# First attention: the value product of an odd key step issued one step later, ahead of the next even step's

## The chip, the cores and the metric

One core of one Trainium2 chip runs the whole program. The metric is device time in microseconds (us) of one execution.

## What is computed

Two post-norm transformer layers over 2048 tokens of width 512, each an attention and a feed-forward block with a residual sum and a layer norm behind each. The change touches only the first layer's attention: 16 heads of 32 dimensions, causal, softmax over scores.

```python
q = jnp.concatenate([q_sem, q_geo], axis=-1)
k = jnp.concatenate([k_sem, k_geo], axis=-1)
scores = jnp.einsum('bhqd,bhkd->bhqk', q, k).astype(jnp.float32) * scale
scores = jnp.where(causal, scores, jnp.finfo(jnp.float32).min)
attn = jax.nn.softmax(scores, axis=-1).astype(v.dtype)
out = jnp.einsum('bhqk,bhkd->bhqd', attn, v)
```

## The kernel before

`layer0_attention` works on 16 **items**, each one chunk of 512 queries and one group of four heads. Item (c, g) has a **step** for each tile of 128 keys that chunk c may see: 4, 8, 12 or 16 steps, 160 in all, an even number in each item. Items 0 to 3 belong to chunk 0, 4 to 7 to chunk 1, 8 to 11 to chunk 2 and 12 to 15 to chunk 3. In an item full tiles and diagonal tiles alternate at first; a diagonal tile covers 512, 384, 256 or 128 queries and gets a mask matmul (line 843).

A step i has this work:

- `scores`: four matmuls on PE, one a head (line 838), each into one of **three** PSUM banks `stb`. ACT takes the exponential of each (line 702) into `probs`, which has four step buffers. Scores number k wait for the exponential of scores k-3.
- `av`, the value product: four matmuls (line 855) that use 32 of the 128 columns each, side by side, and sum into one bank `avb`. They wait for the step's four exponentials.
- POOL adds the probabilities of an odd step to those of the even step before it (line 668), in two halves, after the even step's `av`.
- `den`, the denominators: four matmuls against ones (line 876) on that sum, for even steps only, in the same shape of 32 columns, into another bank.

Beside this runs the search for each query's largest score, which the softmax subtracts, for items still to come. A `unit` is one matmul (line 817) into one of **three** PSUM banks `sbank`, over 512 keys or, on the diagonal, 128 to 512; DVE reduces it (line 740, or 745 on the diagonal). The matmul of a unit waits until the unit three before it is reduced. A `turn` transposes an item's maxima on PE (line 824) after DVE has finished them (line 752), and takes an `sbank` bank too. There are 640 units; all of them have been issued before item 15, the last item, begins.

`attention0_plan` writes out one list, `order`, and every engine walks it and takes its own entries. It first sets which units and turns stand in the gap behind each of the 640 scores (`in_gap`), by costs and due times. Then it lays out the steps: for step i the scores of heads 0, 1 and 2, each with its gap, then the block of 32-column work, then head 3. Before the change that block is `av` of step i-1 at every i, followed by `den` of step i-3 where i is odd. Six entries `prep` (conversions on ACT and DVE that belong to the next stage) are put in the block's place too, in the first steps of item 15; PE has no work in them.

The lines that set the waits are these.

```python
if k >= 3:
    pe.wait_ge(s["exp_ok"], k - 2)
...
pe.wait_ge(s["exp_ok"], 4 * i + 4)
...
act.wait_ge(s["av_ok"], i - PSLOTS + 1)
```

Of the kernel before, what the change touches and what calls it, by code (L numbers as in the profile page):

```python
# [131 lines left out]
def query_slots(items):  # L132

    slot = [n % (QSLOTS + INX) if n < 2 * NG else (n - 2 * NG) % QSLOTS for n in range(items)]
    old = [max((o for o in range(n) if slot[o] == slot[n]), default=-1) for n in range(items)]
    return slot, old
# [305 lines left out]
def attention0_plan():  # L442


    items = [(c, g) for c in range(NC) for g in range(NG)]
    steps, first, final = [], [], []
    for n, (c, g) in enumerate(items):
        diagonal, full = [c * TC + d for d in range(TC)], list(range(c * TC))
        order = [kt for pair in zip(full, diagonal) for kt in pair] + full[TC:] if c else diagonal
        first.append(len(steps))  # L450
        steps += [(n, kt) for kt in order]
        final.append(len(steps) - 1)
    units = [[(h, t, u) for u in (*range(c), c) for t in range(TC) for h in range(GH)] for c, g in items]

    def width(n, kt):
        return CH - max(0, kt - TC * items[n][0]) * P

    def cost(n, unit):
        h, t, u = unit
        return 151 + (CH if u < items[n][0] else (t + 1) * P)  # L460

    clock, begin = 0.0, []
    gaps = []
    for i, (n, kt) in enumerate(steps):
        if i == first[n]:
            begin.append(clock)
        for h in range(4):
            clock += 0.25 * width(n, kt) * 7.0
            gaps.append((clock, i, h))
    lead = 7500.0  # L470
    q_old = query_slots(len(items))[1]

    loads, last_use = [], {}
    for i, (n, kt) in enumerate(steps):
        last_use[n, kt // TC] = i
    for n, (c, g) in enumerate(items):
        loads += [(n, j) for j in range(c + 1)]
    freed = {}
    for at, (n, j) in enumerate(loads):
        freed[n, j] = last_use[loads[at - KSLOTS]] if at >= KSLOTS else -1  # L480

    done = 0.0
    corners = []
    for n in range(len(items)):
        done += sum(cost(n, x) for x in units[n])
        corners.append((begin[n] - lead, done))
    early = list(range(EARLY))
    here, have = 0.0, corners[early[-1]][1]
    path = [(here, have)]
    while have < corners[-1][1]:  # L490
        slope, to = max(((d - have) / (at - here), n) for n, (at, d) in enumerate(corners) if d > have)
        here, have = corners[to]
        path.append((here, have))

    def when(amount):
        for (a0, h0), (a1, h1) in zip(path, path[1:]):
            if amount <= h1:
                return a0 + (a1 - a0) * (amount - h0) / (h1 - h0)
        return path[-1][0]

    in_gap = [[] for _ in gaps]
    before = []
    amount, at_gap = 0.0, 0
    end_of = {i: max(k for k, gap in enumerate(gaps) if gap[1] == i) for i in range(len(steps))}
    for n in range(len(items)):
        for j, unit in enumerate(units[n]):
            amount += cost(n, unit)
            if n in early:
                before.append(("unit", n, j))
                continue  # L510
            t = when(amount)
            free = max(freed[n, unit[2]], final[q_old[n]] if q_old[n] >= 0 else -1)
            if free >= 0:
                t = max(t, gaps[end_of[free]][0] + 4000.0)
            while at_gap < len(gaps) - 1 and gaps[at_gap][0] < t:
                at_gap += 1
            in_gap[at_gap].append(("unit", n, j))
        if n in early:
            if n > 0:
                before.insert(len(before) - len(units[n]) + 4, ("turn", n - 1))  # L520
            if n == early[-1]:
                before.append(("turn", n))
        else:
            k = at_gap
            while gaps[k][0] < gaps[at_gap][0] + 1500.0:
                k += 1
            in_gap[k].append(("turn", n))

    order = list(before)
    k = 0  # L530
    for i, (n, kt) in enumerate(steps):
        for h in range(4):
            if h == 3 and i > 0:
                order.append(("av", i - 1))
                if 2 <= i - final[-2] < 2 + PREP:
                    order.append(("prep", i - final[-2] - 2))
                if i >= 3 and i % 2:
                    order.append(("den", i - 3))
            order.append(("scores", i, h))
            order += in_gap[k]  # L540
            k += 1
    order += [("av", len(steps) - 1), ("den", len(steps) - 2)]
    return items, steps, first, final, units, loads, last_use, order


def layer0_attention(nc, stage_before, stored, landed, qx, qk_dram, m_dram, xs_dram, acc_dram, token, V, X, hi, lo, qst, consts, early, out_w, first_o):
    items, steps, first, final, units, loads, last_use, order = attention0_plan()
    unit_no, ring, scored = {}, {}, {}
    for at, ev in enumerate(order):
# [2025 lines left out]
```

## Time and profile before

| what | value |
|---|---|
| time, median of 3 runs | 2267.35 us (2264.82 to 2269.28) |
| span of the profiled execution, first to last instruction | 2262.5 us |
| what lies around the span, against the median | 4.85 us |
| PE busy in the span | 2168.5 us, 96% |
| DVE, ACT, POOL busy | 52%, 33%, 30% |
| first attention in the span | some 160 to 740 us |

The profiled execution has a span but no separate time of its own beside it; the three runs lie 2.3 to 6.8 us above its span. A busy PE is an upper bound: matmuls overlap in the records, so the pace of a stretch is read from the starts of its instructions, not from their lengths. Idle time of an engine that is not the bottleneck costs nothing.

### The profile page before, as it was taken

What the parts mean: (1) busy time and instruction counts of PE and PEld (TensorE: products, weight loads), DVE (VectorE), ACT (ScalarE), POOL (GpSimd) and SP (SyncE); (2) the same over time, 40 slices, a digit from 0 to 9 for tenths busy, and PEclk for the clock granted to TensorE, in tenths of its full rate; (3) what the DMA queues carried; (4) which work ended last, traced back from release to release, by engine and by line L of the source; (5) the groups of instructions that cost most, each with busy time, mean ns of one, the idle gap of its engine ahead of it and who ended that gap; (6) DMA issues with size and microseconds to landing.
All of it is one profiled execution on the core that took longest, in us unless ns stands there. A gap on an engine that the chain in (4) does not pass through costs nothing. (4 is left out here: it accounts for less than half of the span.)

```text
span 2262.5 us, 27504 instructions
## 1 busy us (share of the span) xinstructions
PE 2168.5 (96%) x10148; PEld 1493.8 (66%) x10148; DVE 1184.8 (52%) x2325; ACT 752.9 (33%) x1351; POOL 669.7 (30%) x456
## 2 busy tenths in 40 slices
PE   7999999999999899999989899999998999999997
PEld 6866555555553554444467778888887888888886
DVE  5877777776662553222246652322336546554666
ACT  3325555555557322111134321111223211211223
POOL 4354555645556105242223250000003021211200
PEclk9989999999999999999999999999999999999999
DMA  4578345333300615555534460000101010100001
GB/s 180 187 200 197 87 123 129 99 91 72 71 17 21 243 65 218 135 120 90 90 104 149 144 231 25 28 19 19 46 1 56 1 38 19 38 19 20 18 19 56
DMA packets 104605, 197.27 MB, mean 87 GB/s; under 512 B 10385, under 2 KB 27665, under 8 KB 103057
## 3 DMA queue, kind: packets, MB, share of 16 engines
q1 hardware_dynamic: 92064, 162.78, 24.4%
q0 software_dynamic: 11408, 29.69, 5.7%
q10 hardware_dynamic: 1008, 3.15, 0.4%
q8 instruction: 78, 1.28, 0.2%
q14 instruction: 47, 0.38, 0.1%
HBM read 123.82 MB, written 71.75 MB: 86 GB/s over the span
## 5 line engine op out<-in xcount | busy, mean ns | idle before, releaser
L702 ACT ACTIVATE a_probs<-a_stb 128x512 f32<-128x512 f32 (+3 forms) x640 | 309.7, 535 | 241.2 <-PE a_stb L843 126.7
L668 POOL TENSOR_TENSOR a_probs<-a_probs 128x1024 f32<-128x1024 f32 (+3 forms) x158 | 278.0, 1773 | 247.9 <-PE a_avb L855 234.0
L740 DVE TENSOR_REDUCE a_mparts<-a_sbank 128x1 f32<-128x512 f32 x384 | 239.9, 683 | 86.3 <-PE a_sbank L817 86.1
L2215 POOL CAST m_wh<-wst 128x1024 fp32r<-128x1024 f32 x24 | 26.7, 1112 | 716.1 <-POOLq L1532 366.9
L57 PE MATMUL m_gu<-hi,m_wh 128*128 128x512 f32 x512 | 199.7, 390 | 3.5 <-DVE lo L2284 1.9
L59 PE MATMUL m_gu<-hi,m_wl 128*128 128x512 f32 x512 | 199.4, 389 | 0.0
L58 PE MATMUL m_gu<-lo,m_wh 128*128 128x512 f32 x512 | 199.2, 389 | 0.0
L855 PE MATMUL a_avb<-a_probs,V 128*32 128x512 f32 (+3 forms) x1280 | 151.7, 546 | 0.7 <-ACT a_probs L702 0.7
L745 DVE CUSTOM_DVE_ANT_0 a_junk<-a_sbank,hidden 128x128 bf16<-128x128 f32 (+3 forms) x256 | 113.1, 487 | 59.0 <-PE a_sbank L817 57.6
L2294 DVE TENSOR_TENSOR m_h<-m_sg,m_gu 128x512 f32<-128x512 f32 x63 | 43.2, 686 | 190.5 <-ACT m_sg L2245 190.3
L2245 ACT ACTIVATE m_sg<-m_gu 128x512 f32<-128x512 f32 x64 | 38.3, 598 | 261.6 <-PE m_gu L59 261.5
L817 PE MATMUL a_sbank<-hi,q 96*128 96x512 f32 (+3 forms) x304 | 118.7, 412 | 5.9 <-DVE a_mparts L740 4.2
L838 PE MATMUL a_stb<-q,hi 97*128 97x512 f32 (+3 forms) x304 | 121.8, 410 | 1.6 <-ACT a_probs L702 1.1
L1817 ACT ACTIVATE pth<-q_tb 128x512 fp32r<-128x512 f32 x64 | 38.2, 598 | 244.6 <-PE q_tb L2074 244.6
L1954 DVE TENSOR_TENSOR ptl<-q_tb,pth 128x512 fp32r<-128x512 f32 x64 | 44.1, 691 | 143.3 <-ACT pth L1817 143.3
L817 PE MATMUL a_sbank<-lo,q 96*128 96x512 f32 (+3 forms) x288 | 109.4, 405 | 5.4 <-DVE a_mparts L740 3.3
L838 PE MATMUL a_stb<-q,lo 97*128 97x512 f32 (+3 forms) x288 | 110.3, 398 | 2.2 <-ACT a_probs L702 1.9
L57 PEld LDWEIGHTS m_gu<-hi,m_wh 128*128 128x128 f32 x512 | 96.1, 188 | 24.0 <-DVE lo L2284 2.1
L59 PEld LDWEIGHTS m_gu<-hi,m_wl 128*128 128x128 f32 x512 | 96.1, 188 | 20.1
L58 PEld LDWEIGHTS m_gu<-lo,m_wh 128*128 128x128 f32 x512 | 96.1, 188 | 19.9
L1303 POOL DMA_INDIRECT acc<-e_rows_b,X x37 | 57.8, 1563 | 166.1 <-DVE e_rows_b L1427 139.2
L57 PE MATMUL q_vb<-vh,pth 128*128 128x512 f32 x256 | 101.3, 396 | 3.7 <-DMA vl<-v 3.7
(289 smaller groups left out, 4753.7 us busy)
## 6 DMA issues: line engine op xcount, KB each, us to landing
qk<-v_hl SPq DMA_DIRECT2D x32, 512.0 KB, 3.1
hi<-qk SPq DMA_DIRECT2D x60, 256.0 KB, 5.2
lo<-qk SPq DMA_DIRECT2D x60, 256.0 KB, 5.3
wst<-in_w_mlp SPq DMA_DIRECT2D x24, 512.0 KB, 3.5
q<-qk SPq DMA_DIRECT2D x42, 256.0 KB, 5.8
xs<-a_zeros POOLq DMA_DIRECT2D x39, 264.0 KB, 2.7
X<-xs SPq DMA_DIRECT2D x39, 264.0 KB, 2.7
v<-vhl SPq DMA_DIRECT2D x16, 512.0 KB, 4.9
```

The lines of the kernel that those rows point to most:

```text
L57: nc.tensor.matmul(out, wh, xh, start=start, stop=False, skip_group_check=True)
L58: nc.tensor.matmul(out, wh, xl, start=False, stop=False, skip_group_check=True)
L59: return nc.tensor.matmul(out, wl, xh, start=False, stop=stop, skip_group_check=True)
L668: nc.gpsimd.tensor_tensor(probs[:, i % PSLOTS, hs, w0:], probs[:, i % PSLOTS, hs, w0:], probs[:, (i + 1) % PSLOTS, hs, w0:], ALU.add)\
L702: nc.scalar.activation(probs[:, i % PSLOTS, h, w0:], stb[:, k % 3, w0:], ACT.Exp, scale=SCALE0)\
L740: nc.vector.reduce_max(to, sbank[:, b, :], AX).then_inc(s["unit_max"], 1)
L745: nc.vector.tensor_tensor_reduce(out=junk[:, k % 2, 0:w], in0=sbank[:, b, 0:w], in1=hidden[:, CH - w:CH], scale=1.0, scalar=BIG, op0=ALU.a ...
L817: nc.tensor.matmul(bank[:, 0:w], qs[q_slot[n]][0:96, h, t * P:(t + 1) * P], kst[at % KSLOTS][0:96, h, 0:w], start=True, stop=True)\
L838: last = nc.tensor.matmul(stb[:, k % 3, w0:], kst[slot_of[n, kt // TC] % KSLOTS][0:97, h, kt % TC * P:(kt % TC + 1) * P], qs[q_slot[n]][0: ...
L855: last = nc.tensor.matmul(avb[HD0 * h:HD0 * (h + 1), w0:], V[:, kt, g * P + h * HD0:g * P + (h + 1) * HD0], probs[:, i % PSLOTS, h, w0:], ...
L1303: nc.gpsimd.indirect_dma_start(acc_dram[:, :], bass.IndirectOffsetOnAxis(ap=to[:, j:j + 1], axis=0), y[:, j % 2, :], None, compute_op=ALU. ...
L1954: nc.vector.tensor_tensor(ptl[:, 4 * g:4 * g + 4, :].rearrange("p a b -> p (a b)"), tb[:, (g + 1) % 2, :], f32(pth[:, 4 * g:4 * g + 4, :]) ...
```

## The change

In `attention0_plan` the block of step i now depends on whether i is odd. For odd i it holds `av` of step i-2, `av` of step i-1 and `den` of step i-3. For even i it is empty, unless step i-1 is the last of its item: then that step's `av` stands there as before. The counter of gaps is renamed.

```diff
     order = list(before)
-    k = 0
+    gap = 0
     for i, (n, kt) in enumerate(steps):
         for h in range(4):
             if h == 3 and i > 0:
-                order.append(("av", i - 1))
+                if i % 2:
+                    order += [("av", k) for k in (i - 2, i - 1) if k >= 0 and k not in final]
+                elif i - 1 in final:
+                    order.append(("av", i - 1))
                 if 2 <= i - final[-2] < 2 + PREP:
                     order.append(("prep", i - final[-2] - 2))
                 if i >= 3 and i % 2:
                     order.append(("den", i - 3))
             order.append(("scores", i, h))
-            order += in_gap[k]
-            k += 1
+            order += in_gap[gap]
+            gap += 1
```

Of the 80 odd steps 16 are the last of an item, so 64 value products move. Only PE's order changes; DVE, ACT, POOL and the DMA queues have their entries in the order they had. Lines behind the edit stand three higher in the changed kernel: 838 becomes 841, 817 becomes 820, 855 becomes 858, 876 becomes 879.

The first place is PE in item 10, steps 80 to 83, all full tiles. `a_stb` are scores, `a_sbank` units, `a_avb` a value product, `a_den` denominators. Before:

```order
L838 MATMUL a_stb<-q,hi 128x512
L817 MATMUL a_sbank<-hi,q 128x512
L855 MATMUL a_avb<-a_probs,V 32x512 x4
L838 MATMUL a_stb<-q,hi 128x512
L817 MATMUL a_sbank<-hi,q 128x512
L838 MATMUL a_stb<-q,hi 128x512
L817 MATMUL a_sbank<-lo,q 128x512 x2
L838 MATMUL a_stb<-q,hi 128x512
L817 MATMUL a_sbank<-lo,q 128x512
L838 MATMUL a_stb<-q,hi 128x512
L817 MATMUL a_sbank<-lo,q 128x512
L855 MATMUL a_avb<-a_probs,V 32x512 x4
```

After the change, the same stretch of PE's program:

```order
L841 MATMUL a_stb<-q,hi 128x512
L820 MATMUL a_sbank<-hi,q 128x512
L841 MATMUL a_stb<-q,hi 128x512
L820 MATMUL a_sbank<-hi,q 128x512
L841 MATMUL a_stb<-q,hi 128x512
L820 MATMUL a_sbank<-lo,q 128x512 x2
L841 MATMUL a_stb<-q,hi 128x512
L820 MATMUL a_sbank<-lo,q 128x512
L841 MATMUL a_stb<-q,hi 128x512
L820 MATMUL a_sbank<-lo,q 128x512
L858 MATMUL a_avb<-a_probs,V 32x512 x8
L879 MATMUL a_den<-a_probs,a_ones 32x512 x4
```

The first `av` (step 81) has moved behind the second group of scores and units and stands as one block of eight with that of step 82. Between two blocks there are now eight scores and nine units in a row, where there were four and four, then four and five.

The second place is PE in item 15, steps 152 to 155, which has no units. Before:

```order
L838 MATMUL a_stb<-q,hi 128x512 x4
L855 MATMUL a_avb<-a_probs,V 32x512 x4
L838 MATMUL a_stb<-q,hi 128x512 x4
L855 MATMUL a_avb<-a_probs,V 32x512 x4
L876 MATMUL a_den<-a_probs,a_ones 32x512 x4
```

After the change:

```order
L858 MATMUL a_avb<-a_probs,V 32x512 x8
L879 MATMUL a_den<-a_probs,a_ones 32x512 x4
L841 MATMUL a_stb<-q,hi 128x512 x8
L858 MATMUL a_avb<-a_probs,V 32x512 x8
L879 MATMUL a_den<-a_probs,a_ones 32x512 x4
```

Here eight scores follow each other with nothing between them, where there were two groups of four.

## Rows read from the trace of the kernel before

**Rows 1.** The page: span, busy time of each engine, granted TensorE clock in 40 slices.

```profile
span 2262.5 us, 27504 instructions
...
PE 2168.5 (96%) x10148; PEld 1493.8 (66%) x10148; DVE 1184.8 (52%) x2325; ACT 752.9 (33%) x1351; POOL 669.7 (30%) x456
...
PEclk9989999999999999999999999999999999999999
```

**Rows 2.** Busy us of each engine by stretch, then clock, DMA share, GB/s.

```profile
692.00:740.00 48.00, 43.97 (x280) 16.46 (x280) 9.28 (x10) 32.04 (x67) 29.54 (x16) 1.00 0.03 10
200.00:690.00 490.00, 475.01 (x2961) 253.27 (x2964) 340.17 (x809) 273.20 (x569) 272.44 (x184) 1.00 0.38 91
```

**Rows 3.** Waits from 175 to 735 us: total us, times, longest.

```profile
DVE a_mparts L740 <- PE a_sbank L817: 86.1, 78, 2.7
...
PEld a_sbank L817 <- DVE a_mparts L740: 19.8, 47, 1.4
```

**Rows 4.** Timeline of PE, item 10: start, us, instructions.

```profile
466.05 0.49 PE L817 MATMUL a_sbank<-hi,q 96*128 96x512 f32 x1
466.48 1.07 PE L855 MATMUL a_avb<-a_probs,V 128*32 128x512 f32 x8
467.36 1.04 PE L876 MATMUL a_den<-a_probs,a_ones 128*32 128x512 f32 x8
468.33 0.50 PE L838 MATMUL a_stb<-q,hi 97*128 97x512 f32 x1
468.67 0.40 PE L817 MATMUL a_sbank<-hi,q 96*128 96x512 f32 x1
...
470.07 0.39 PE L817 MATMUL a_sbank<-hi,q 96*128 96x512 f32 x1
470.39 1.07 PE L855 MATMUL a_avb<-a_probs,V 128*32 128x512 f32 x8
471.39 0.50 PE L838 MATMUL a_stb<-q,hi 97*128 97x512 f32 x1
...
472.91 0.50 PE L817 MATMUL a_sbank<-lo,q 96*128 96x512 f32 x1
...
473.50 0.50 PE L817 MATMUL a_sbank<-lo,q 96*128 96x512 f32 x1
473.94 1.06 PE L855 MATMUL a_avb<-a_probs,V 128*32 128x512 f32 x8
...
475.79 0.50 PE L838 MATMUL a_stb<-q,hi 97*128 97x512 f32 x1
```

**Rows 5.** Timeline of DVE in the same stretch.

```profile
469.10 2.48 DVE L740 TENSOR_REDUCE a_mparts<-a_sbank 128x1 f32<-128x512 f32 x4 [1.31 <-PE a_sbank L817]
472.16 3.08 DVE L740 TENSOR_REDUCE a_mparts<-a_sbank 128x1 f32<-128x512 f32 x5 [0.57 <-PE a_sbank L817]
```

**Rows 6.** Groups of full width from 175 to 735 us: count, busy us, mean ns.

```profile
L702 ACT ACTIVATE a_probs<-a_stb 128x512 f32<-128x512 f32 x443 | 240.0, 600 | 136.0 <-PE a_stb L838 107.7 <-PE a_stb L843 25.5
L740 DVE TENSOR_REDUCE a_mparts<-a_sbank 128x1 f32<-128x512 f32 x384 | 239.9, 683 | 86.3 <-PE a_sbank L817 86.1
```

**Rows 7.** Timeline of PE in item 15.

```profile
729.22 0.98 PE L838 MATMUL a_stb<-q,hi 97*128 97x512 f32 x3
730.42 0.50 PE L838 MATMUL a_stb<-q,hi 97*128 97x512 f32 x1 [0.21 <-ACT a_probs L702]
730.85 1.06 PE L855 MATMUL a_avb<-a_probs,V 128*32 128x512 f32 x8
...
735.31 0.50 PE L838 MATMUL a_stb<-q,hi 97*128 97x512 f32 x1
```

**Rows 8.** Timeline of ACT in item 15.

```profile
729.76 2.07 ACT L702 ACTIVATE a_probs<-a_stb 128x512 f32<-128x512 f32 x4 [1.41 <-PE a_stb L838]
```

**Rows 9.** Timeline of POOL in item 15.

```profile
728.61 4.71 POOL L668 TENSOR_TENSOR a_probs<-a_probs 128x1024 f32<-128x1024 f32 x2 [1.38 <-PE a_avb L855]
```

**Rows 10.** One line's instructions: the `prep` conversions on ACT, ns min/median/max.

```profile
L718 ACT ACTIVATE woh<-V x4: 632/652/653, 694.4 to 702.8; 128x512 fp32r<-128x512 f32 x4
```

## The prediction

> **What bounds the kernel now.** I read the page first, then the busy time by stretch, then the waits, then the timelines of two places. The page shows PE busy for 96% of the span and the clock granted nearly in full [rows 1]. By stretch, in the first attention the clock is 1.00, PE is busy 475 of 490 us between 200 and 690 us, DVE 340, ACT 273 and POOL 272 [rows 2]. So PE sets the pace there, but DVE, at 69%, is not far behind. The waits say the same: DVE waits for units (86 us in all), while PE's weight loads waited 20 us for reductions, in 47 places [rows 3]. Those 47 places matter below: with three banks DVE already stops PE where units come close together. In the last item the picture is another: no units, ACT busy 32 of 48 us [rows 2], and PE waits for an exponential at the fourth scores of every step [rows 7].
>
> **What a seam costs.** The change removes no instruction. It removes 64 seams, the places where PE goes from full-width matmuls to 32-column ones and back. In item 10 a seam is read from starts [rows 4]. Six matmuls go from 468.67 to 470.07: 0.233 us each. From the last unit to the value product it is 0.32 (470.07 to 470.39), 0.09 more. A value product that scores follow takes 1.00 (470.39 to 471.39); one that 32-column work follows takes 0.88 (466.48 to 467.36); 0.12 more. The first scores behind a block hold the next unit off for 0.34 (468.33 to 468.67), 0.11 more. Together **0.32 us a seam**, and 64 of them are 20.5 us, the ceiling of what can come.
>
> The Trainium skill, "TensorEngine Tiling (Array Packing)", section "Tiling Modes", says that changing the tiling mode drains the TensorE. The row's 0.32 us agrees with that. By that rule alone the change would take off the whole 20.5 us.
>
> **What the seam was hiding.** While PE runs a block, DVE and ACT empty the three banks each has ahead. The change puts eight scores, with all their units, in one run. A unit goes with each scores at 2 x 0.233 = 0.467 us, and a reduction follows the one before it after (2.48 - 0.68)/3 = 0.60 us [rows 5, 6]. So a run of full units falls behind by 0.13 us a unit, and three banks cover only the first few.
>
> *Nine full units (item 10, steps 81 to 83).* The run begins at 468.33, its first four units at 468.67 to 470.07 as before, the first reduction at 469.10 [rows 4, 5]. Reduction n ends at 469.10 + 0.60(n-1) + 0.68, and the unit three later starts 0.06 us after that (before: reduction 2 of the second run ends at 472.16 + 0.60 + 0.68 = 473.44, its unit starts at 473.50). Unit 5 would come at 470.07 + 0.47 = 470.54, reduction 2 allows 470.44: no wait. Unit 6 would come at 471.01, allowed 471.04. From here DVE sets the pace: unit 7 at 471.64, 8 at 472.24, 9 at 472.84. Behind a delayed unit the block starts 0.44 later (473.50 to 473.94), not 0.32: 473.28. The merged block is 0.88 + 0.88 + 0.97 (467.36 to 468.33): the next scores at 476.01. Before they came at 475.79 [rows 4]. So this merge is **0.22 us slower**, although its seam is gone.
>
> *Eight full units.* The same walk ends with unit 8 at 472.24, the block at 472.68, the next scores at 475.41. Before, two groups of four without a wait are 468.33 + 2.06 + 1.00 + 2.06 + 1.85 = 475.30. So 0.11 us slower.
>
> *Few or narrow units.* With five or fewer there is no wait, and the merge gives 0.32.
>
> **The sum.** I counted in the order what each of the 64 merged runs of eight scores holds, a narrow unit by its share of 512.
>
> - 21 runs hold less than seven full units' worth. Between -0.32 and nothing; narrow diagonal scores, which let PE run faster than DVE and ACT, are in 20 of them, so I take half: -0.16 x 21 = -3.4 us.
> - 36 hold seven or more, nine of them with a turn, at which PE waits for the maxima anyway, so that a late DVE is partly paid already. Between -0.32 and +0.22; most are like the eight-unit walk, the ones with a turn or narrow units below it. I take +0.07: +2.5 us.
> - 7 lie in the last item. Eight scores from 729.22: the first exponential starts at 729.76, four take 2.07 with the last one 0.60 long, so 0.49 apart [rows 6, 8]; the fifth ends at 729.76 + 1.96 + 0.60 = 732.32. Scores 8 wait for it, plus 0.06 (730.36 to 730.42 before): 732.38. The block starts 0.43 later [rows 7], 732.81, and the next scores at + 2.73 = 735.54, against 735.31 before: +0.23 each, 1.6 us. In addition three of the six `prep` conversions, 0.65 us each on ACT [rows 10], now stand in the middle of a run where ACT sets the pace, no block being there to cover them. Between nothing and 0.65; I take 0.5: +1.5 us. Together +3.1.
>
> The sum is -3.4 + 2.5 + 3.1 = **+2.2 us**. It is made against the profiled span of 2262.5, which has no other time of its own on the page; the median of the runs is 4.85 above it, and I put the sum on the median: 2269.5 us.
>
> **What costs nothing, and why.** The moved product's own waits: its exponentials are a step older than before. Exponentials that reuse a buffer wait for the product of four steps before, which now stands two steps ahead of them, not three: still PE time of a whole block and more. POOL's sum of a pair starts behind the even step's product, which comes 0.88 later in its block, but `den`, which needs it, comes 0.88 later too; in the last item the sum ends at 728.61 + 4.71 = 733.32, and `den`, which ends 0.97 later at 735.31, begins at 734.34 [rows 7, 9], so 1.0 us is left. DVE's, ACT's, POOL's and the DMA queues' orders do not change. The clock is already 1.00 [rows 2]. Behind the attention nothing is touched.
>
> **The rivals.**
>
> 1. *The seams come off whole.* PE is busy 97% of 200 to 690 us [rows 2], and if DVE's banks hold more than I walked, the 57 merges with units give 57 x -0.32 = -18.2; with +3.1 in the last item 2267.35 - 15.1 = 2252.2 us. Half way, light runs -0.32 and heavy ones -0.1 (-6.7 - 3.6 + 3.1), it is 2260.1. Against it: the five-unit run in which PE stands at 472.91 and 473.50 for reductions, after only three units [rows 4, 5]. The Trainium skill's rule ("TensorEngine Tiling (Array Packing)", "Tiling Modes") speaks for this rival. Chance 0.13.
> 2. *DVE's three banks become the bound* (slower). If nearly all 36 heavy runs go as the nine-unit walk, and a wait in the light ones eats their gain, it is 36 x 0.22 + 0 + 3.1 = 11.0: 2278.4 us. It decides once the light runs give less than about 0.05 us each and the heavy ones cost more than 0.1: -1.1 + 3.6 + 3.1 is already 5.6. For it: 0.60 against 0.467 us a unit. Against it: many of the heavy runs count narrow units, which DVE takes faster. Chance 0.23.
> 3. *The change doesn't do what it says.* The order shows the blocks of eight, so this has no chance of its own.
>
> **How the numbers follow.** The runs shown spread over 4.5 us, 0.2% of the time, and about 0.2% is what a measurement of this kernel can tell from no change. The forecast, within that, has 0.64; slower by more 0.23; faster by more 0.13. The range 2262 to 2276 holds the whole of "no change" (2262.8 to 2271.9), and on the upper side most of rival 2, whose end is 2278.4; the deep half of rival 1 and the top of rival 2 are left out, under 2 in 10.
>
> **What would show it.** Right: the merged block with its second product 0.88 behind the first; the pair of steps in item 10 (466.48 to 473.94 before, 7.46 long) at about 7.7; the total wait of units for reductions clearly above 20 us; in item 15 a period of 6.3 where it was 6.09 (729.22 to 735.31), with PE waiting at scores 4 to 8. Wrong: no growth of those waits in item 10, and items 8 to 14 some 2 us shorter each; or a wait of `den` for POOL, which I priced at nothing.

## The result and the profile after

The changed kernel took 2275.81 us (median of 5 runs, 2268.42 to 2279.14) against 2266.36 us before, a ratio of 1.0039 (95% interval 1.0023 to 1.0055): slower. Two later comparisons, 12 runs of it each, gave 1.0025 (1.0008 to 1.0041) and 1.0017 (1.0003 to 1.0031). All three show a loss, but not its size: by the intervals it is 5.2 to 12.5, 1.8 to 9.3 and 0.7 to 7.0 us, and the last two hold the 2.2 us forecast. By the first comparison, 9.4 us, the case is the second one, slower; the medians of the later two, 3.1 and 3.9 us above, lie within the 4.5 us that the prediction calls no change.

The profiled run is the fastest of the first five, 2268.42 us with a span of 2266.6. Its page and two stretches, to set beside [rows 1, 2]:

```profile
span 2266.6 us, 27504 instructions
...
PE 2168.4 (96%) x10148; PEld 1500.8 (66%) x10148; DVE 1179.4 (52%) x2325; ACT 752.6 (33%) x1351; POOL 669.2 (30%) x456
...
PEclk9989999999999999999999999999999999999999
```

```profile
692.00:740.00 48.00, 44.46 (x261) 17.24 (x259) 7.07 (x9) 31.59 (x68) 29.73 (x16) 1.00 0.06 18
200.00:690.00 490.00, 471.66 (x2959) 258.38 (x2959) 336.74 (x810) 272.40 (x568) 271.93 (x184) 0.99 0.37 91
```

The span is 4.1 us longer. Between 200 and 690 us PE is busy 471.66 us, 3.35 less than before, and the granted clock is 0.99 where it was 1.00. The waits between 175 and 735 us, against [rows 3]:

```profile
DVE a_mparts L743 <- PE a_sbank L820: 86.8, 46, 3.9
...
PEld a_sbank L820 <- DVE a_mparts L743: 35.5, 106, 1.4
```

Weight loads of units wait 35.5 us for reductions, in 106 places, where it was 19.8 us in 47. The nine-unit run of item 10, on PE and then on DVE, against [rows 4, 5]:

```profile
471.05 0.50 PE L841 MATMUL a_stb<-q,hi 97*128 97x512 f32 x1
471.39 0.39 PE L820 MATMUL a_sbank<-hi,q 96*128 96x512 f32 x1
...
473.26 0.41 PE L820 MATMUL a_sbank<-hi,q 96*128 96x512 f32 x1
...
473.85 1.01 PE L820 MATMUL a_sbank<-lo,q 96*128 96x512 f32 x2
...
474.96 0.50 PE L820 MATMUL a_sbank<-lo,q 96*128 96x512 f32 x1
...
475.56 0.49 PE L820 MATMUL a_sbank<-lo,q 96*128 96x512 f32 x1
475.98 1.92 PE L858 MATMUL a_avb<-a_probs,V 128*32 128x512 f32 x16
477.72 1.04 PE L879 MATMUL a_den<-a_probs,a_ones 128*32 128x512 f32 x8
478.69 0.50 PE L841 MATMUL a_stb<-q,hi 97*128 97x512 f32 x1
```

```profile
471.82 5.47 DVE L743 TENSOR_REDUCE a_mparts<-a_sbank 128x1 f32<-128x512 f32 x9 [1.54 <-PE a_sbank L820]
```

DVE reduces nine units without a pause, (5.47 - 0.68)/8 = 0.60 us apart. The fifth unit (473.26) comes without a wait, the sixth (473.85) with one, and from there PE keeps DVE's pace. The merged block, 475.98 to 478.69, takes 2.71. From the first scores to the next ones behind the block it is 478.69 - 471.05 = 7.64 us, against 475.79 - 468.33 = 7.46 before: 0.18 slower. Item 15, on PE and on ACT, against [rows 7, 8]:

```profile
726.58 0.50 PE L841 MATMUL a_stb<-q,lo 97*128 97x512 f32 x1
726.92 0.63 PE L841 MATMUL a_stb<-q,hi 97*128 97x512 f32 x2
727.77 2.46 PE L841 MATMUL a_stb<-q,hi 97*128 97x512 f32 x5 [0.22 <-ACT a_probs L705]
730.16 1.92 PE L858 MATMUL a_avb<-a_probs,V 128*32 128x512 f32 x16
731.90 1.04 PE L879 MATMUL a_den<-a_probs,a_ones 128*32 128x512 f32 x8
732.87 0.96 PE L841 MATMUL a_stb<-q,hi 97*128 97x512 f32 x3
```

```profile
727.12 4.03 ACT L705 ACTIVATE a_probs<-a_stb 128x512 f32<-128x512 f32 x8 [2.26 <-PE a_stb L841]
```

The period is 732.87 - 726.58 = 6.29 us where it was 6.09; ACT works through eight exponentials in a row, and PE waits for it from the fourth scores on.

So the places look as they were walked. What remained to be found is why the runs of the first comparison lose more than the places do.

### The profile page after: what moved, and what is told of

Its sections match the earlier page's. It is cut to its first block and busy times, and to the rows that moved or that the text cites. A ratio compares the mean times of both kernels' runs of the same rounds, so it can differ in the third digit from the quotient of the medians.

```text
span 2266.6 us, 27504 instructions
## 1 busy us (share of the span) xinstructions
PE 2168.4 (96%) x10148; PEld 1500.8 (66%) x10148; DVE 1179.4 (52%) x2325; ACT 752.6 (33%) x1351; POOL 669.2 (30%) x456
## 5 line engine op out<-in xcount | busy, mean ns | idle before, releaser
L858 PE MATMUL a_avb<-a_probs,V 128*32 128x512 f32 (+3 forms) x1280 | 139.5, 545 | 0.7 <-ACT a_probs L705 0.7
L820 PE MATMUL a_sbank<-hi,q 96*128 96x512 f32 (+3 forms) x304 | 125.6, 435 | 7.1 <-DVE a_mparts L743 5.0
L57 PE MATMUL m_yb<-m_wh,m_hh 128*128 128x512 f32 x256 | 101.4, 396 | 4.3 <-DVE X L2301 4.3
```

The costliest lines, as they stand in the source:

```text
L57: nc.tensor.matmul(out, wh, xh, start=start, stop=False, skip_group_check=True)
L820: nc.tensor.matmul(bank[:, 0:w], qs[q_slot[n]][0:96, h, t * P:(t + 1) * P], kst[at % KSLOTS][0:96, h, 0:w], start=True, stop=True)\
L858: last = nc.tensor.matmul(avb[HD0 * h:HD0 * (h + 1), w0:], V[:, kt, g * P + h * HD0:g * P + (h + 1) * HD0], probs[:, i % PSLOTS, h, w0:], ...
```

## The experiments

Each time stands beside runs of the kernel before on the same chip: 23, 34 and 35 of them in the three batches, medians 2264.83, 2264.79 and 2264.43 us, and in each batch a granted clock of 0.984 in the mean over the runs. The kernels that merge a part use one rule:

```diff
+    def late(k):
+        return k % 2 == 1 and k not in final and ...
...
-                if i % 2:
-                    order += [("av", k) for k in (i - 2, i - 1) if k >= 0 and k not in final]
-                elif i - 1 in final:
-                    order.append(("av", i - 1))
+                order += [("av", k) for k, moved in ((i - 2, True), (i - 1, False))
+                          if k >= 0 and late(k) == moved]
```

**Items 0 to 14 alone**: the rule ends in `k < first[-1]`.

> The 57 merges of items 0 to 14, item 15 as before. Theory (a seam is worth 0.32 us, given back by waits for DVE's banks): by the traces the 21 light merges give -2.5 us and the heavy ones about as much back, so without the 3.0 us of the last item the trace is within 1.5 us of the kernel before, where the granted clock does not fall more often. Rival 1 (the last item alone makes the change slow): 2266 us or less. Rival 2 (the clock falls to its lower level more often in items 0 to 14, since PE now stands still in longer runs): 2270 to 2274 us, with a mean clock below 0.983.

2263.66 us, ratio 0.9995 (0.9985 to 1.0005), mean clock 0.9835: no difference. Rival 2 is out as it was put; rival 1's figure fits here, but the next run does not bear it out.

**Item 15 alone**: the rule ends in `k > first[-1]`.

> The 7 merges of item 15 alone. Theory: +3.0 us, from ACT, which sets the pace of the runs of eight scores: 2269.4 us, mean clock as before (0.985). Rival 1 (the last item makes the whole loss): +9 us. In the trace item 15 has the period 6.29 us of the changed kernel, where it was 6.09.

2267.87 us, ratio 1.0011 (1.0000 to 1.0022), 3.0 us above: the size that ACT's pace gives, not 9.

**The reductions halved**, in the changed kernel and, with a rule that ends in `False`, in the old order. Both leave out the maximum of half of each full unit.

```diff
-                        nc.vector.reduce_max(to, sbank[:, b, :], AX).then_inc(s["unit_max"], 1)
+                        nc.vector.reduce_max(to, sbank[:, b, 0:CH // 2], AX).then_inc(s["unit_max"], 1)
```

> The changed kernel with full units reduced over 256 of their 512 columns, so that DVE needs about 0.35 us instead of 0.60 for one (the maximum of the other half is left out). To be compared with e4. Theory: without the waits for banks the 57 merges give their 0.32 us, and the last item still costs 3.0: about 15 us faster than e4. Rival (the merge itself gives nothing, or the clock takes it): within 4 us of e4.

> The kernel before with the same half reductions (the maximum of the other 256 columns of a full unit is left out): the bar for e3. PE's order is that of the kernel before, in which waits for reductions are few, so it should be 3 to 10 us below 2266 us.

The old order took 2254.82 us (5 runs), the new one 2249.35 (6 runs): 5.5 us faster by the medians, 7.0 by the means, less than the 15 expected. The trace says where the rest is. Waits, and the nine-unit run of item 10, in the new order:

```profile
PEld a_sbank L821 <- DVE a_mparts L744: 8.0, 18, 1.1
```

```profile
463.19 0.50 PE L842 MATMUL a_stb<-q,hi 97*128 97x512 f32 x1
...
467.37 1.92 PE L859 MATMUL a_avb<-a_probs,V 128*32 128x512 f32 x16
469.11 1.04 PE L880 MATMUL a_den<-a_probs,a_ones 128*32 128x512 f32 x8
470.08 0.50 PE L842 MATMUL a_stb<-q,hi 97*128 97x512 f32 x1
```

The run that took 7.64 us takes 6.89, and no unit in it waits. Weight loads of units wait 8.0 us for reductions in the new order and 7.2 in the old one; with whole reductions the merges had raised this from 19.8 to 35.5. From one `den` to the next, most heavy merges (seven full units' worth or more) now gain 0.31 to 0.36 us each: that with whole reductions the banks eat the seams is shown. From the old order's trace to the new one's, 35 of the 36 heavy merges give 9.1 us, the light ones 4.5 (20 of the 21: the first has no `den` ahead of it to measure from, here and below). Against that stand the one heavy merge left, which meets a fall of the clock and loses 3.3, and item 15, which loses 4.9 here (its first merge alone 2.99). That leaves 5.4 in these traces of the 15 expected. Two steps of that expectation failed: not every merge gives the whole seam, and item 15 and the clock cost more than they were put at; the mean clock over the runs was 0.981, against 0.984 for the old order.

**The changed kernel again**, unaltered.

> The changed kernel once more, unaltered, on the chip and in the rounds of the three others. By its parts (items 0 to 14 alone ran 1.2 us below the kernel before, the last item alone 3.0 us above it) it should be 1.8 us above the kernel before; by its first comparison 9.4 us above. Theory A (the parts add up, and the first comparison met more falls of the clock): 0 to 5 us above, mean clock about 0.983. Theory B (both parts together make the clock fall more): 7 to 11 us above, mean clock about 0.980.

Ratio 1.0025 (1.0008 to 1.0041), median 3.1 us above, mean 4.8, with a mean clock of 0.9815: between the two theories, A by the time, B by the clock.

**Only merges that pay**: 29 of them, none in item 15.

```diff
+        return k % 2 == 1 and k not in final and k in (1, 9, 17, 19, 21, 33, 37, 41, 45, 53, 63, 65, 67, 75, 87, 91, 93, 99, 101, 107, 109, 115, 117,
+                                                          123, 125, 131, 133, 139, 141)
```

> Only 29 of the 64 merges: those whose run of eight scores leaves DVE time for its units, or ends at a turn at which PE waits anyway; none in item 15. Theory (each merge gives 0.32 us where no bank is waited for): 29 merges, some with part of the gain, 6.5 us below the kernel before. Rival (the gain is eaten by the clock or by a later wait): within 2 us of it.

**2256.72 us**, ratio 0.9971 (0.9960 to 0.9983), 8.1 below the kernel before: it beats both kernels. The seam is worth its price where the run leaves DVE time. Not all of the 8.1 need be the merges': in the profile they give 6.4 us from `den` to `den`, and a fall of the clock at one of them, told of below, takes 2.8 back. The profile's span is 10.5 below that of the kernel before, 7.0 of it behind the attention, where the program is the same.

**PE kept busy in item 15**:

```diff
                     last.then_inc(s["st_ok"], 1)
+                    if n == NI - 1 and i < final[-1]:
+                        nc.tensor.matmul(sbank[:, h % 3, w0:],
+                                         kst[slot_of[n, kt // TC] % KSLOTS][0:96, h, kt % TC * P:(kt % TC + 1) * P],
+                                         qs[q_slot[n]][0:96, h, w0:], start=True, stop=True)
```

> The changed kernel with one more matmul behind each scores of item 15, into the free unit banks, whose result nobody reads: PE has work where it waited for ACT. The period of item 15 should be about 6.45 us instead of 6.29, some 1 us in all. Theory (PE's waits in item 15 let the clock fall there and behind): no fall of the clock in item 15, mean clock up, time equal to or below a2_again. Rival (the falls have nothing to do with item 15's waits): 1 us above a2_again, mean clock the same.

2270.69 us, ratio 1.0026 (1.0015 to 1.0038), mean clock 0.9829. That is 2.8 us above the changed kernel on the same chip by the medians, but 0.7 by the means, with a clock 0.0014 higher: the two can't be told apart. Item 15 itself, from its first scores to the last `den`, takes 2.6 us longer than in the first profile of the changed kernel, not the 1 us expected. So the run does not settle the theory that PE's waits in item 15 bring the clock down. Against it stands that in the three profiles of the changed kernel there is no fall to explain in that item: the granted clock was 1.00 from 691 to 742 us in each.

**The conversions at the blocks**:

```diff
-                if 2 <= i - final[-2] < 2 + PREP:
-                    order.append(("prep", i - final[-2] - 2))
+                if i % 2 and 2 <= i - final[-2] < 2 + PREP:
+                    order += [("prep", i - final[-2] - 2), ("prep", i - final[-2] - 1)]
```

> The changed kernel with the six conversions on ACT moved in pairs to the steps that hold a block, where they stood one in each of six steps. Theory (a conversion in the middle of a run of eight scores is not covered): the first three merges of item 15 fall from +0.87, +0.65 and +0.43 us to about +0.2 each, 1.2 us in all; the whole time falls by 1.2 us, too little to be told. Rival (the narrow diagonal scores cost it): the three stay as they are.

The second and third merges of item 15 fell from +0.65 and +0.43 us to +0.13 and -0.09. ACT's timeline shows the pairs between the runs of exponentials:

```profile
702.12 1.14 ACT L721 ACTIVATE woh<-V 128x512 fp32r<-128x512 f32 x2
705.92 3.37 ACT L705 ACTIVATE a_probs<-a_stb 128x384 f32<-128x384 f32 x8 [2.65 <-PE a_stb L846]
709.18 1.14 ACT L725 ACTIVATE oth<-X 128x512 fp32r<-128x512 f32 x2
```

The first merge cannot be judged: in this profile the clock is at its lower level from 700 us on, just there. The whole, 1.0009 (0.9997 to 1.0021), can't be told from no change.

**The parts and the whole side by side**, and a kernel without any merge in which only what stands behind the attention comes later:

```diff
                     start, stop = i == first[n], i == final[n]
+                    if i == final[-1]:
+                        for k in range(15):
+                            nc.tensor.matmul(sbank[:, k % 3, :], kst[slot_of[n, kt // TC] % KSLOTS][0:96, 0, 0:P],
+                                             qs[q_slot[n]][0:96, 0, :], start=True, stop=True)
                     pe.wait_ge(s["exp_ok"], 4 * i + 4)
```

> The changed kernel, unaltered, beside its two parts in the same rounds on one chip, which the earlier comparisons did not have. Theory A (the parts add up): its excess over the kernel before is the sum of those of e1_second and e2_second, within 2 us. Theory B (together they make the clock fall more than each alone): 3 us or more above that sum, with a mean clock 0.0015 or more below theirs.

> The 57 merges of items 0 to 14 once more. Theory A: within 2 us of the kernel before, and the mean clock within 0.001 of it. Theory B: the same, since the clock falls more only with item 15.

> The 7 merges of item 15 once more: 3 us above the kernel before under both theories, mean clock within 0.001 of it.

> The kernel before with 15 matmuls more ahead of its last value product, into the free unit banks, whose result nobody reads: no merge, but everything behind the attention comes about 3.5 us later. Theory (the excess comes from waits in the attention itself): 3.5 us above the kernel before, mean clock the same. Rival (any shift of the later stages makes the clock fall more often): 6 us or more above it, mean clock lower by 0.0015.

| kernel | median us | above before (mean) | ratio, 95% | mean clock |
|---|---|---|---|---|
| changed | 2268.28 | 3.9 (4.4) | 1.0017 (1.0003 to 1.0031) | 0.9820 |
| items 0 to 14 | 2263.90 | -0.5 (-0.7) | 0.9996 (0.9981 to 1.0011) | 0.9834 |
| item 15 | 2269.03 | 4.6 (4.2) | 1.0024 (1.0007 to 1.0041) | 0.9836 |
| 15 matmuls more | 2271.44 | 7.0 (6.6) | 1.0028 (1.0013 to 1.0044) | 0.9818 |

The parts add up: -0.5 + 4.6 is 4.1, the whole 3.9. By the time theory A holds; the clock, 0.0014 and 0.0016 below that of the two parts, stands about at the mark set for theory B. The last row is the surprise. Its 15 matmuls, on PE:

```profile
742.88 0.50 PE L838 MATMUL a_stb<-q,hi 97*128 97x512 f32 x1
743.22 3.58 PE L853 MATMUL a_sbank<-q,hi 96*128 96x512 f32 x15
746.73 1.06 PE L859 MATMUL a_avb<-a_probs,V 128*32 128x512 f32 x8
```

They put off the last `den` by 2.7 us, since PE would have waited 0.69 there anyway, and the runs lose 7.0 us (2.9 to 10.0 by the interval), with a mean clock as low as that of the changed kernel. By these figures the rival has it; but the profile does not bear out that the rest is lost behind the attention. It is 10.7 us longer than that of the kernel before. Of these, 7.8 stand already at the first scores of item 2, where the two programs are still the same, and only 0.4 are added behind the last `den`. The stretch in which they come, with the 15 matmuls and then in the kernel before:

```profile
154.00:200.00 46.00, 44.41 (x165) 29.21 (x165) 28.63 (x118) 12.18 (x27) 19.64 (x17) 0.52 0.80 179
```

```profile
154.00:200.00 46.00, 43.84 (x220) 28.97 (x220) 34.08 (x128) 16.18 (x39) 26.49 (x23) 0.74 0.81 182
```

The granted clock was 0.52 against 0.74, some 550 us ahead of the edit. The first profile of item 15 alone is likewise 5.9 us late before its first merge. So it is not shown that a later start makes the clock fall more often in the stages behind; why these twelve runs lose more than 2.7 us stays open.

**One fall of the clock inside the attention.** In all eight profiles of kernels with merges in items 0 to 14 and whole reductions the clock goes from 2.4 to 1.2 GHz for some 6.8 us, from a point between 324 and 328 us on, at the head of item 7. The third profile of the changed kernel shows it, and below it stands the kernel before:

```profile
318.00:326.40 8.40, 7.25 (x47) 4.03 (x45) 7.55 (x16) 4.75 (x10) 4.17 (x3) 1.00 0.96 223
326.40:333.20 6.80, 6.80 (x29) 4.85 (x33) 4.10 (x22) 3.17 (x6) 2.62 (x3) 0.50 0.11 43
```

```profile
318.00:326.40 8.40, 7.26 (x47) 4.29 (x48) 7.56 (x17) 4.73 (x9) 4.24 (x2) 1.00 0.93 214
326.40:333.20 6.80, 6.80 (x47) 3.85 (x45) 3.94 (x21) 3.46 (x8) 4.22 (x5) 1.00 0.11 41
```

PE was busy 7.25 of the 8.4 us ahead of it, in the kernel before 7.26: neither busy time nor the waits tell the two apart: up to 327 us PE stands once for a bank, for 1.1 us, in both. In the fall it does 29 matmuls in 6.8 us instead of 47, and the merge there costs 2.7 to 2.9 us in each of the eight. Of the five profiles whose order there is the old one, a single one (item 15 alone, the first) has a fall near, shorter, at 331 us. Why the merges bring it on stays open.

The Trainium skill ("TensorE: Matmul & The Clock Gate", section "A second HAM failure mode: psum-queue depth-cycling") tells of a kernel whose clock swung between its two levels because TensorE idled briefly and often while it cycled through PSUM banks. More waits for banks, 106 places for 47, would fit that; at this place the waits ahead of the fall are those of the kernel before, so no run here shows it to be the cause.

## Why the prediction was right or wrong

The range held the time of the first comparison, by 0.2 us at its upper end, and there the likeliest case did not come; by the medians of the later two it did. Step by step, from one `den` to the next in the third profile of the changed kernel against the one before:

- **The seam, 0.32 us**: right. The merges that gain most gain 0.30 to 0.35, and with halved reductions most heavy ones do too. Runs of five full units without a turn, walked at the whole 0.32, gave 0.24 to 0.25. The measured seam agrees with the Trainium skill's rule that a change of tiling mode drains TensorE ("TensorEngine Tiling (Array Packing)", "Tiling Modes"). The 20.5 us for all seams did not come, because the longer run asks more of the other engines.
- **The walks**: right in kind. The nine-unit run is 0.18 slower (0.22 walked). Eight full units were walked at +0.11; the runs that hold eight came out between -0.08 and +0.08 where no turn lies in them.
- **21 light merges**, -3.4 us forecast: -2.45.
- **36 heavy merges**, +2.5 forecast: +2.6, by luck, for the cause is another. Of it 2.75 is the fall of the clock near 326 us. Without that merge the other 35 make -0.2. The term of +0.07 each was too high: four of the nine runs with a turn gained all 0.32.
- **Item 15**, +3.1 forecast: +2.9, made of +0.20 each for the plain merges (0.23 walked) and the conversions in the middle of a run, which moving them confirms for two of three.
- **"The clock is already 1.00"**, a term put at nothing: this is the step that failed. With the merges comes a fall of the clock near 326 us, in eight of eight profiles, and the merge it meets costs 2.75 us. Without it the places sum to some -2.45 - 0.2 + 2.9 = +0.3 us, with it to +3.0. That this lies near the +2.2 forecast is luck: what the heavy merges were priced too high is about what the fall took. The later comparisons, 4.8 and 4.4 us in the mean, allow +3.0 within their intervals. The first comparison's 9.4 us are not accounted for: its profile is that of its fastest run, and the mean clock of its five runs was 0.980. Over the 12 runs of the changed kernel in the last batch, 0.001 of clock goes with 1.8 us, so the 0.0021 by which its mean lies below that of the kernel before goes with 3.8; which falls make this up was not found, since each execution has its own and only one of each set was profiled.
- **"Behind the attention nothing is touched"** is not refuted. From the last `den` to the end the three profiles of the changed kernel take 0.3 us more, 3.2 less and 2.8 more than the one of the kernel before: no direction.
- **Rival 2** named DVE's banks as what would make it slower. The banks take the gain away, as the halved reductions show, but they do not make the loss. In the first comparison the side was rival 2's; the mechanism was not.
- **Rival 1**, the seams whole, is what halved reductions let one see in part: -10.2 us in the merges of items 0 to 14, -13.5 without the one that met a fall of the clock, where whole seams are -18.2.

## What to carry to other kernels

Taking out a switch of the array's tiling is worth its 0.32 us only where the other engines keep pace over the longer run that it leaves: count what one run asks of each ring of banks (0.60 against 0.467 us a unit here, three banks), and merge only where they cover it. A bound engine at 97% can lose what it gains when the work between its blocks is doubled in length. And when a change of a few us is forecast, the granted clock belongs in the sum: here one fall at one merge, 2.75 us, outweighed all the other terms together (+0.3). One profile tells of its own execution alone, so before a loss is put down to a stage, see from where on the trace runs late.

## What was not expected

- A fall of the clock to 1.2 GHz in steady work with PE 86% busy ahead of it (7.25 of 8.4 us), costing 2.7 to 2.9 us, in eight of eight profiles of one family of orders.
- Two profiles of kernels with the same program up to there differ by 7.8 us at the first scores of item 2 already, with a granted clock of 0.52 and 0.74 from 154 us on.
